# Layer 0's first stage: row normalisation with Newton's inverse root on VectorE instead of a square root on ScalarE

## The chip, the cores and the metric

One core of a Trainium2 chip runs the whole program. The metric is the device time of one launch in microseconds, the median of several runs.

## The reference, cut to what matters

Two layers, each a graph block and a block of eight experts with two chosen per token, over x of 128 x 64 x 128 (8192 tokens of 128 numbers). What the change touches is the end of layer 0's graph block, the normalisation behind it, and the routing:

```python
def _layernorm(x, axis=-1, eps=1e-05):
    m = jnp.mean(x, axis=axis, keepdims=True)
    v = jnp.var(x, axis=axis, keepdims=True)
    return (x - m) / jnp.sqrt(v + eps)

x = x + _L0_gnn_ref(_layernorm(x), adj, W1, b1, W2, b2)   # U (relu((U^T x) W1 + b1) W2 + b2), U: eigenvectors
x = x + _L0_ffn_ref(_layernorm(x), router_w, w1, w2, w3)
# _L0_ffn_ref: logits = flat @ router_w.T; softmax; top_k of 2; gates renormalised (+ 1e-9);
#              out = sum of the gates times w2 (silu(w1 x) * w3 x) of the two experts
x = x + _L1_gnn_ref(_layernorm(x), adj, ...)
x = x + _L1_ffn_ref(_layernorm(x), ...)
```

## The kernel before, in words

The eigenvectors of the graph's Laplacian are computed first (to about 291 us). Then comes the stage of the change, `gnn0_*`, which runs over 16 tiles (`TILES`) of 512 tokens, each tile four blocks (`PAIRS`) of 128 rows. It is a software pipeline of 21 steps (`A0_STEPS`). Each engine has its own list, written out by hand for every step `s`, and runs it strictly in order; semaphores tie the lists together.

- TensorE in step s: the multiplication with U^T (L1192) for tile s; the counting of a routing group (`count`, L948 and L949); w2 (L1201) for tile s-1; the transposes (L1209) of the normalised tile s-3, which wait for `a0_xh2`; w1 (L1215) for tile s; the output multiplication with U (L1220) for tile s-1; the logits (L861) of tile s-3.
- ScalarE in step s: first the square root (L1232) of the variance of tile s-2, then the copies out of PSUM: `ga` (L1237), `gm` (L1242), `xT` (L1247), then the Relu `gh` (L1252), and in every second step the Exp of the gates (L937, L939).
- VectorE in step s: the reciprocal of the root (L1321) and the scaling (L1270, four instructions) of tile s-2; the residual add (L1280, from PSUM) of tile s-1, its `bn_stats` (L1287) and `bn_aggr` (L1295), and the variance plus epsilon (L1301). With `T = s-2` and `T1 = s-1`, `old` and `new` say whether these tiles exist.
- GpSimd: the 16 additions of a bias row (L1367), then the sends: one indirect DMA (L1012) for each of the 64 blocks of rows, which scatters the normalised rows to their slots in memory. `scatter` waits for the slots and the gates of a group; up to group 4 `rest` also waits for `a0_xadd` and `a0_xT` of later steps. SP issues nothing in this stage; it waits for all 64 sends before it loads the first expert tile.

The routing works in eight groups of two tiles (`GROUPS`, `GT`). Steps 5, 7, ... 19 are *choosing* steps: `choose` is a chain of 13 links on small operands (128 x 64 or 128 x 128), each of which waits for the one before it on VectorE's own semaphore; the kernel hands it a function `beside(k)` that puts other instructions behind link k, ahead of the wait for it. At its end stands `picked` (L923), for which the count on TensorE waits. Steps 6, 8, ... 20 are *placing* steps: `place` takes the slots from the count, and `gates` the gates, again with `beside`. Steps 0 to 4 have no routing.

```python
def due(s, lag):
    g, rest = divmod(s - lag, GT)
    return [g] if rest == 0 and 0 <= g < GROUPS else []
```

After the stage come the 71 expert tiles of layer 0, then layer 1, whose routing uses the same `Router` and whose normalisation keeps its square root.

Of the kernel before, what the change touches and what calls it, by code (L numbers as in the profile page):

```python
# [6 lines left out]
I32 = mybir.dt.int32  # L7
# [828 lines left out]
class Router:  # L836
# [114 lines left out]
    def place(self, dve, own, g):  # L951
# [6 lines left out]
        n1 = own.inc(V.tensor_tensor(r["a"], self.rank[:, 0:one], r["o1"], ALU.mult))  # L958
        n2 = own.inc(V.tensor_tensor(r["b"], self.rank[:, (self.ways - 1) * one:self.ways * one], r["o2"], ALU.mult))
        dve.wait_ge(own.sem, n1)  # L960
        with self.nc.allow_low_precision(reason="whole numbers below 2**24"):
            V.tensor_reduce(self.t["slot"][:, 0, qs], group(r["a"]), AX.X, ALU.add).then_inc(s("slots"), 1)
            dve.wait_ge(own.sem, n2)
            V.tensor_reduce(second[:, qs], group(r["b"]), AX.X, ALU.add).then_inc(s("slots"), 1)

# [160 lines left out]

def first_norm_sum(nc, act, S, E, t, i):
# [129 lines left out]
def gnn0_dve(nc, dve, own, S, t, ps, route):  # L1257
# [4 lines left out]
    for s in range(A0_STEPS):  # L1262
# [4 lines left out]
        def scaled(q):  # L1267
            if not old:
                return
            ins = V.tensor_scalar(t["pay"][:, T * PAIRS + q, 0:P], X[:, T * PAIRS + q, :], t["mv"][:, q, 0:1],  # L1270
                                  t["sd"][:, 2, q:q + 1], ALU.subtract, ALU.mult)
            if q == PAIRS - 1:
                ins.then_inc(S("a0_xh2"), 1)

# [14 lines left out]
        def moments(q):  # L1289
            if not new:  # L1290
                return
            if q == 0 and old:
                dve.wait_ge(S("a0_xh2"), T + 1)
            dve.wait_ge(S("a0_stats"), T1 * PAIRS + q + 1)
            V.bn_aggr(t["mv"][:, q, :], t["bn"][:, q, :]).then_inc(S("a0_moments"), 1)  # L1295

        def variance():
# [15 lines left out]
        def by_gates(k):  # L1313
            if k == 0:
# [4 lines left out]
        if old:  # L1319
            dve.wait_ge(S("a0_root"), T + 1)  # L1320
            own.chain(V.reciprocal(t["sd"][:, 2, :], t["sd"][:, 1, :]))  # L1321
        if due(s, GT + 3):
            route.choose(dve, own, due(s, GT + 3)[0], by_choice)
            moments(3)
            variance()
        else:
            for q in range(PAIRS):
                scaled(q)
            if due(s, GT + 4):
                route.place(dve, own, due(s, GT + 4)[0])  # L1330
                route.gates(dve, own, due(s, GT + 4)[0], by_gates)
            else:
                added()
                for q in range(PAIRS - 1):
                    stats(q)
            stats(PAIRS - 1)
            for q in range(PAIRS):
                moments(q)
            variance()
# [644 lines left out]
def build(nc, d, out, scratch):  # L1984

    with ExitStack() as ctx:
# [45 lines left out]
        t["bn"], t["mv"], t["sd"] = sb("bn", [P, PAIRS, 6]), sb("mv", [P, PAIRS, 2]), sb("sd", [P, 3, PAIRS])  # L2032
        nm = sb("norm", [P, 2, 2, PAIRS])
# [191 lines left out]
```

## Time and profile before

| what | value |
|---|---|
| timed runs, us | 1470.77, 1477.38, 1479.84; median 1477.38 |
| span of the profiled execution, us | 1487.3 |
| instructions | 23954 |
| busy: TensorE, VectorE, ScalarE, GpSimd | 76%, 61%, 39%, 44% |
| mean granted clock of TensorE | 0.919 |

The profiled execution is one run of its own; its span goes from the first to the last instruction. The busy shares are means over the whole program; the stage in question is a small part of it, about 292 to 449 us.

### The profile page before, as it was taken

To read this page: it belongs to the slowest core of one execution; us is meant where nothing else is said; L and a number is where in the kernel's file an instruction comes from. 1 tells how busy PE (TensorE), PEld (TensorE's weight loads), DVE (VectorE), ACT (ScalarE), POOL (GpSimd) and SP (SyncE) were. 2 spreads that over 40 slices of the span, in tenths; PEclk is the share of its full clock that TensorE was granted. 3 is DMA by queue.
4 is the path that set the end of the run, shared out by engine and by line. 5 is a ranking of instruction groups with operands and counts; after the bars stand their busy time and mean duration, and the time that the engine had idled before them with its cause. 6 is when DMAs were issued, how large, how long until landed. Compare 5 with 4: busy or idle time off the path is not lost.

```text
span 1487.3 us, 23954 instructions
## 1 busy us (share of the span) xinstructions
PE 1130.7 (76%) x6500; PEld 939.8 (63%) x6500; DVE 904.2 (61%) x3700; ACT 574.8 (39%) x1601; POOL 655.7 (44%) x675
## 2 busy tenths in 40 slices
PE   4555685488716877889999587899878877799990
PEld 3555674366615766668888443677657666699990
DVE  5776788667753534446677687888434423355673
ACT  3556566045411211112222266577523322244440
POOL 3000000145565665655444770044456656556654
PEclk9999999989856988899999799899999979799995
DMA  9993000001112221222243330001112212122436
GB/s 228 428 427 132 1 1 1 0 1 33 37 43 62 68 65 56 62 59 63 64 117 108 117 127 15 1 31 34 33 49 68 67 55 64 61 70 69 131 106 226
DMA packets 59269, 125.57 MB, mean 84 GB/s; under 512 B 13132, under 2 KB 39637, under 8 KB 57600
## 3 DMA queue, kind: packets, MB, share of 16 engines
q0 software_dynamic: 20000, 73.21, 13.1%
q1 hardware_dynamic: 39136, 50.84, 12.6%
q8 instruction: 53, 0.87, 0.2%
q14 instruction: 80, 0.66, 0.1%
HBM read 50.83 MB, written 74.99 MB: 85 GB/s over the span
## 4 chain that ended last, share of the span: by engine, by line
PE 56%; issue 15%; DVE 14%; another core or an unknown queue 5%; ACT 5%; DMA 2%; POOL 1%; DVEq 0%; SPq 0%; ACTq 0%; POOLq 0%
PE bank L1583 15%; PE bank L1574 9%; PE bank L1572 6%; PE bank L1571 6%; PE bank L1796 3%; PE bank L195 3%; PE bank L1804 3%; PE bank L1751 2%; PE bank L1559 2%; DMA u<-planes 1%; DVE bnh L1648 1%; DVE u L180 1%; DVE u L171 1%; DVE bn L1119 1%
## 5 line engine op out<-in xcount | busy, mean ns | idle before, releaser
L1426 POOL DMA_INDIRECT planes<-work,goal x284 | 301.5, 1062 | 217.0 <-DVE work L1495 133.0
L1012 POOL DMA_INDIRECT rows<-pay,slot x256 | 259.5, 1014 | 259.9 <-issue 82.9
L1583 PE MATMUL bank<-pay 128*128 128x128 f32 (+1 forms) x1988 | 297.9, 290 | 61.2 <-issue 25.7
L1583 PEld LDWEIGHTS bank<-pay 128*128 128x128 f32 (+1 forms) x1988 | 273.0, 200 | 89.1 <-issue 36.1
L1543 ACT ACTIVATE pay<-bank,pay 128x256 f32<-128x256 f32 x284 | 126.6, 475 | 214.7 <-PE bank L1574 119.9
L1539 ACT ACTIVATE pay<-bank 128x256 f32<-128x256 f32 (+1 forms) x213 | 80.7, 383 | 311.2 <-PE bank L1572 216.5
L1574 PE MATMUL bank<-pay 128*128 128x256 f32 x568 | 145.3, 402 | 10.1 <-issue 8.8
L1571 PE MATMUL bank<-pay 128*128 128x256 f32 (+1 forms) x426 | 138.2, 408 | 12.9 <-issue 12.3
L1516 DVE TENSOR_TENSOR pay<-pay,bank 128x256 f32<-128x256 f32 (+1 forms) x213 | 88.2, 418 | 95.4 <-ACT pay L1539 58.3
L1572 PE MATMUL bank<-pay 128*128 128x256 f32 (+1 forms) x426 | 135.6, 402 | 0.0
L1574 PEld LDWEIGHTS bank<-pay 128*128 128x128 f32 x568 | 109.9, 204 | 25.2 <-issue 10.2
L195 PE MATMUL bank<-u 63*64 63x2 f32 (+61 forms) x496 | 73.6, 255 | 67.2 <-DVE u L180 66.2
L1468 DVE COPY pay<-wreg 128x1066 f32 (+1 forms) x142 | 103.3, 727 | 27.3 <-issue 26.7
L1478 DVE COPY pay<-bank 128x256 f32<-128x256 f32 x142 | 59.7, 421 | 83.7 <-remote 55.7
L195 PEld LDWEIGHTS bank<-u 63*64 63x64 f32 (+61 forms) x496 | 64.4, 217 | 72.7 <-DVE u L180 71.4
L1572 PEld LDWEIGHTS bank<-pay 128*128 128x128 f32 (+1 forms) x426 | 81.6, 192 | 19.4 <-issue 1.4
L1571 PEld LDWEIGHTS bank<-pay 128*128 128x128 f32 (+1 forms) x426 | 76.1, 193 | 27.0 <-issue 15.9
L1804 PE MATMUL bank<-wreg,work 128*128 128x128 f32 x512 | 69.6, 282 | 20.4 <-ACT work L1863 17.5
L1804 PEld LDWEIGHTS bank<-wreg,work 128*128 128x128 f32 x512 | 63.4, 194 | 31.6 <-ACT work L1863 22.3
L1490 DVE TENSOR_TENSOR pay<-bank,pay 128x256 f32<-128x256 f32 x71 | 30.1, 424 | 75.4 <-PE bank L1583 51.8
L714 POOL MEMSET work<- 128x868 f32 x1 | 0.8, 822 | 166.4 <-DVE u L350 166.4
L1796 PE MATMUL bank<-u,wreg 128*128 128x512 f32 x128 | 65.9, 618 | 0.0
(409 smaller groups left out, 2006.6 us busy)
## 6 DMA issues: line engine op xcount, KB each, us to landing
rows<-pay POOLq DMA_DIRECT2D x10, 3432.0 KB, 56.1
pay<-rows SPq DMA_DIRECT2D x142, 130.0 KB
u<-planes SPq DMA_DIRECT2D x64, 256.0 KB, 4.9
planes<-work,goal POOLq DMA_INDIRECT x284
wreg<-in_w SPq DMA_DIRECT2D x1, 4264.0 KB, 24.9
wreg<-in_w SPq DMA_DIRECT2D x1, 4112.0 KB, 13.2
X<-in_x SPq DMA_DIRECT2D x2, 2048.0 KB, 20.4
rows<-pay,slot POOLq DMA_INDIRECT x256
```

Source lines behind the costliest of these rows:

```text
L195: T.matmul(out, A[0:rows, col:col + 1].to_broadcast([rows, N]), rhs, start=True, stop=True).then_inc(hp, 1)
L1012: return self.nc.gpsimd.indirect_dma_start(out=xs, out_offset=bass.IndirectOffsetOnAxis(ap=self.t["slot"][:, k, q:q + 1], axis=0), in_=sel ...
L1426: nc.gpsimd.indirect_dma_start(out=planes, out_offset=bass.IndirectOffsetOnAxis(ap=t["goal"][:, j * 2 + h:j * 2 + h + 1], axis=0), in_=t[" ...
L1468: V.tensor_copy(t["wst"][j % 2][:, 0:WB[layer]], W[:, bass.ds(expert * WB[layer], WB[layer])]).then_inc(s("w"), 1)
L1516: V.tensor_tensor(t["hh"][c][0:w, :], t["hs"][c][0:w, :], ps[c][0:w, TS:2 * TS], ALU.mult).then_inc(s("hh"), 1)
L1543: A.activation(t["hh"][c], ps[c][:, 0:TS], ACT.Gelu, bias=t["wst"][j % 2][:, 2 * CH1 * P + c:2 * CH1 * P + c + 1]).then_inc(s("hh"), 1)
L1571: T.matmul(ps[c][0:n, 0:TS], w[:, a:a + n], x, start=True, stop=True)
L1572: T.matmul(ps[c][0:n, TS:2 * TS], w[:, HID0 + a:HID0 + a + n], x, start=True, stop=True).then_inc(s("up"), 1)
L1574: T.matmul(ps[c][:, 0:TS], w[:, c * P:(c + 1) * P], x, start=True, stop=True).then_inc(s("up"), 1)
L1583: ins = T.matmul(ps[4 + j % 2][:, h * P:(h + 1) * P], t["hh"][c][0:n, h * P:(h + 1) * P], t["wst"][j % 2][0:n, at + c * P:at + (c + 1) * P ...
L1796: T.matmul(ps[2 + c % 2][:, :], t["WS"][:, c * P:(c + 1) * P], t["x1"][i], start=True, stop=True).then_inc(S("a1_up"), 1)
L1804: ins = T.matmul(ps[4 + 2 * (i % 2)][:, q * P:(q + 1) * P], t["sh"][c][:, q * P:(q + 1) * P], t["WS"][:, (CH1 + c) * P:(CH1 + c + 1) * P], ...
```

## The change

In layer 0's first stage the square root on ScalarE and the reciprocal on VectorE are replaced by a bit-pattern start value and three Newton steps, 11 small operations (128 x 4) on VectorE per tile: operation 0 takes the place of the variance plus epsilon at the end of the step, operations 1 to 10 stand in the next step. In a choosing step they go behind links 0 to 9, in a placing step behind the operations of `place` and `gates`, in steps without routing one behind the other ahead of the add. The four scalings move to behind links 10 to 12, or to the end of the step; the four `bn_aggr` move to the very end and write into two buffers in turn.

```diff
+ROOT_OPS = 11
+SEED = 0x5f3759df - (1 << 22) - (1 << 31)
+
+def inverse_root(V, dve, t, sem, n, k, mv=None):
+    mv = t["mv"] if mv is None else mv
+    half, y, q = (t["sd"][:, i, :] for i in range(3))
+    if k:
+        dve.wait_ge(sem, n * ROOT_OPS + k)
+    if k == 0:
+        ins = V.tensor_scalar(half, mv[:, :, 1], EPS, 0.5, ALU.add, ALU.mult)
+    elif k == 1:
+        ins = V.tensor_scalar(t["sdi"][:, 1, :], t["sdi"][:, 0, :], -0.5, float(SEED), ALU.mult, ALU.add)
+    elif k % 3 == 2:
+        ins = V.tensor_tensor(q, y, y, ALU.mult)
+    elif k % 3 == 0:
+        ins = V.tensor_tensor(q, q, half, ALU.mult)
+    else:
+        ins = V.scalar_tensor_tensor(out=y, in0=q, scalar=-1.5, in1=y, op0=ALU.add, op1=ALU.mult)
+    ins.then_inc(sem, 1)
...
 def gnn0_act(nc, act, S, t, ps, route):
...
-        if 2 <= s < TILES + 2:
-            act.wait_ge(S("a0_var"), s - 1)
-            A.activation(t["sd"][:, 1, :], t["sd"][:, 0, :], ACT.Sqrt).then_inc(S("a0_root"), 1)
...
         def scaled(q):
...
+            if q == 0:
+                dve.wait_ge(S("a0_inv"), (T + 1) * ROOT_OPS)
+            ins = V.tensor_scalar(t["pay"][:, T * PAIRS + q, 0:P], X[:, T * PAIRS + q, :], t["mvs"][T % 2][:, q, 0:1],
+                                  t["sd"][:, 1, q:q + 1], ALU.subtract, ALU.mult)
...
+        def root(k):
+            if old and 1 <= k < ROOT_OPS:
+                inverse_root(V, dve, t, S("a0_inv"), T, k)
...
         def variance():
...
             dve.wait_ge(S("a0_moments"), (T1 + 1) * PAIRS)
-            V.tensor_scalar(t["sd"][:, 0, :], t["mv"][:, :, 1], EPS, None, ALU.add).then_inc(S("a0_var"), 1)
+            if old:
+                dve.wait_ge(S("a0_xh2"), T + 1)
+            inverse_root(V, dve, t, S("a0_inv"), T1, 0, t["mvs"][T1 % 2])
 
         def by_choice(k):
-            if k <= 3:
-                scaled(k)
-            elif k == 5:
+            root(k + 1)
+            if k == 5:
                 added()
             elif 6 <= k <= 9:
                 stats(k - 6)
-            elif k >= 10:
-                moments(k - 10)
+            elif k == 10:
+                scaled(0)
+                scaled(1)
+            elif k >= 11:
+                scaled(k - 9)
+
+        def by_place(k):
+            root(k + 2)
 
         def by_gates(k):
+            root(k + 6)
             if k == 0:
                 added()
             else:
                 stats(k - 1)
 
-        if old:
-            dve.wait_ge(S("a0_root"), T + 1)
-            own.chain(V.reciprocal(t["sd"][:, 2, :], t["sd"][:, 1, :]))
         if due(s, GT + 3):
             route.choose(dve, own, due(s, GT + 3)[0], by_choice)
-            moments(3)
-            variance()
-        else:
+        elif due(s, GT + 4):
+            root(1)
+            route.place(dve, own, due(s, GT + 4)[0], by_place)
+            route.gates(dve, own, due(s, GT + 4)[0], by_gates)
+            root(10)
+            stats(PAIRS - 1)
             for q in range(PAIRS):
                 scaled(q)
...
+        else:
+            for k in range(1, ROOT_OPS):
+                root(k)
+            added()
             for q in range(PAIRS):
-                moments(q)
-            variance()
+                stats(q)
+            for q in range(PAIRS):
+                scaled(q)
+        for q in range(PAIRS):
+            moments(q)
+        variance()
```

`place` gets the same argument `beside` as `gates` has, and calls it behind each of its four operations.

## Rows read from the trace of the kernel before

**Rows 1.** GpSimd's sends, the view of line L1012 and GpSimd's order of time.

```profile
L1012 POOL DMA_INDIRECT rows<-pay,slot x64: 969/974/1592, 339.0 to 446.9; - x64
...
410.28 0.97 POOL L1012 DMA_INDIRECT rows<-pay,slot  x1 [0.30 <-issue]
...
437.35 1.59 POOL L1012 DMA_INDIRECT rows<-pay,slot  x1 [6.88 <-issue]
```

**Rows 2.** VectorE in order of time, at its longest wait.

```profile
428.45 0.22 DVE L873 COPY rt<-bank 128x64 f32<-128x64 f32 x1 [9.41 <-remote]
```

**Rows 3.** All engines in order of time, step 7's add to step 8's.

```profile
341.83 0.68 DVE L1280 TENSOR_TENSOR X<-X,bank 128x512 f32<-128x512 f32 x1
...
345.09 0.26 DVE L923 TENSOR_TENSOR rt<-rt,carry 128x128 f32<-128x128 f32 x1
...
345.41 0.49 PE L948 MATMUL bank<-rt,kroute 128*128 128x128 f32 x2 [1.97 <-DVE rt L923]
...
345.79 0.57 ACT L1237 COPY u<-bank 128x512 f32<-128x512 f32 x1
...
347.29 1.02 PE L1215 MATMUL bank<-u,small 128*128 128x512 f32 x2
...
348.14 1.02 PE L1220 MATMUL bank<-u,UTB 128*128 128x512 f32 x2
...
349.20 0.69 DVE L1280 TENSOR_TENSOR X<-X,bank 128x512 f32<-128x512 f32 x1 [1.17 <-PE bank L1220]
```

**Rows 4.** VectorE in order of time, from step 6's add to step 7.

```profile
336.30 0.69 DVE L1280 TENSOR_TENSOR X<-X,bank 128x512 f32<-128x512 f32 x1 [2.56 <-PE bank L1220]
...
338.73 0.17 DVE L1301 TENSOR_SCALAR sd<-mv 128x4 f32<-128x4 f32 x1
339.17 0.18 DVE L1321 RECIPROCAL sd<-sd 128x4 f32<-128x4 f32 x1 [0.27 <-ACT sd L1232]
339.39 0.22 DVE L873 COPY rt<-bank 128x64 f32<-128x64 f32 x1
```

**Rows 5.** Waits from 290 to 450 us: total, times, longest.

```profile
PE bank L1215 <- ACT u L1237: 5.9, 6, 2.4
```

**Rows 6.** Busy time of each engine in one stretch, granted clock.

```profile
core 0: us, PE busy (x) PEld busy (x) DVE busy (x) ACT busy (x) POOL busy (x), PEclk, DMA share, GB/s
...
329.00:410.30 81.30, 63.72 (x364) 49.38 (x362) 61.51 (x330) 41.65 (x75) 39.97 (x41) 0.92 0.10 33
```

**Rows 7.** VectorE in order of time, the links of step 7.

```profile
341.38 0.27 DVE L889 TENSOR_TENSOR rt<-rt,rc 128x64 f32<-128x64 f32 x1
341.69 0.22 DVE L892 SCALAR_TENSOR_TENSOR rt<-rt 128x64 f32<-128x64 f32 x1
...
342.80 0.15 DVE L898 TENSOR_TENSOR rc<-rc 128x8 f32<-128x8 f32 x1
342.87 0.27 DVE L899 TENSOR_TENSOR rt<-rt,rc 128x64 f32<-128x64 f32 x1
...
343.94 0.26 DVE L908 TENSOR_TENSOR rt<-rt,rc 128x64 f32<-128x64 f32 x1
...
344.24 0.42 DVE L915 TENSOR_TENSOR_SCAN rt<-kroute,rt 128x128 f32<-128x128 f32 x1
...
344.69 0.29 DVE L918 TENSOR_TENSOR rt<-rt 128x128 f32<-128x128 f32 x1
...
346.13 1.12 DVE L1270 TENSOR_SCALAR pay<-X,mv,sd 128x128 f32<-128x128 f32 x4
347.17 0.22 DVE L958 TENSOR_TENSOR rt<-bank,rt 128x64 f32<-128x64 f32 x1
```

**Rows 8.** VectorE in order of time, steps 2 and 5.

```profile
304.75 4.47 DVE L1270 TENSOR_SCALAR pay<-X,mv,sd 128x128 f32<-128x128 f32 x4
...
327.53 0.68 DVE L1280 TENSOR_TENSOR X<-X,bank 128x512 f32<-128x512 f32 x1
```

**Rows 9.** ScalarE in order of time, a table load and the next root.

```profile
386.99 1.28 ACT L1232 ACT_TABLE_LOAD   x1
388.28 0.20 ACT L1232 ACTIVATE sd<-sd 128x4 f32<-128x4 f32 x1
```

More of the change, by code:

```diff
@@ L949, in count, with place @@
         T.matmul(self.rank, ones, r["e"][:, 0:self.ways * E8 * GQ], start=False, stop=True).then_inc(self.s("rank"), 1)
-    def place(self, dve, own, g):
+    def place(self, dve, own, g, beside=lambda k: None):
         V, r, s, c = self.nc.vector, self.t["rt"], self.s, self.t["rc"]
@@ L958, in place @@
         n1 = own.inc(V.tensor_tensor(r["a"], self.rank[:, 0:one], r["o1"], ALU.mult))
+        beside(0)
         n2 = own.inc(V.tensor_tensor(r["b"], self.rank[:, (self.ways - 1) * one:self.ways * one], r["o2"], ALU.mult))
+        beside(1)
         dve.wait_ge(own.sem, n1)
@@ L962, in place @@
             V.tensor_reduce(self.t["slot"][:, 0, qs], group(r["a"]), AX.X, ALU.add).then_inc(s("slots"), 1)
+            beside(2)
             dve.wait_ge(own.sem, n2)
             V.tensor_reduce(second[:, qs], group(r["b"]), AX.X, ALU.add).then_inc(s("slots"), 1)
+            beside(3)
     def gates(self, dve, own, g, beside=lambda k: None):
@@ L1269, in scaled @@
                 return
-            ins = V.tensor_scalar(t["pay"][:, T * PAIRS + q, 0:P], X[:, T * PAIRS + q, :], t["mv"][:, q, 0:1],
-                                  t["sd"][:, 2, q:q + 1], ALU.subtract, ALU.mult)
+            if q == 0:
+                dve.wait_ge(S("a0_inv"), (T + 1) * ROOT_OPS)
+            ins = V.tensor_scalar(t["pay"][:, T * PAIRS + q, 0:P], X[:, T * PAIRS + q, :], t["mvs"][T % 2][:, q, 0:1],
+                                  t["sd"][:, 1, q:q + 1], ALU.subtract, ALU.mult)
             if q == PAIRS - 1:
                 ins.then_inc(S("a0_xh2"), 1)
+        def root(k):
+            if old and 1 <= k < ROOT_OPS:
+                inverse_root(V, dve, t, S("a0_inv"), T, k)
         def added():
@@ L1291, in moments @@
                 return
-            if q == 0 and old:
-                dve.wait_ge(S("a0_xh2"), T + 1)
+            if q == 0 and T1 >= 2:
+                dve.wait_ge(S("a0_xh2"), T1 - 1)
             dve.wait_ge(S("a0_stats"), T1 * PAIRS + q + 1)
-            V.bn_aggr(t["mv"][:, q, :], t["bn"][:, q, :]).then_inc(S("a0_moments"), 1)
+            V.bn_aggr(t["mvs"][T1 % 2][:, q, :], t["bn"][:, q, :]).then_inc(S("a0_moments"), 1)
         def variance():
@@ L1317, in by_gates @@
                 stats(k - 1)
-        if old:
-            dve.wait_ge(S("a0_root"), T + 1)
-            own.chain(V.reciprocal(t["sd"][:, 2, :], t["sd"][:, 1, :]))
         if due(s, GT + 3):
             route.choose(dve, own, due(s, GT + 3)[0], by_choice)
-            moments(3)
-            variance()
-        else:
+        elif due(s, GT + 4):
[4 more added lines that the diff above has]
+            stats(PAIRS - 1)
             for q in range(PAIRS):
                 scaled(q)
[L1329 to L1336, printed above, removed]
-            for q in range(PAIRS):
-                moments(q)
-            variance()
+        else:
+            for k in range(1, ROOT_OPS):
+                root(k)
+            added()
+            for q in range(PAIRS):
+                stats(q)
[4 more added lines that the diff above has]
+        variance()
 def clear_rows(nc, pool, S, zeros, xs):
@@ L2032, in build @@
         t["bn"], t["mv"], t["sd"] = sb("bn", [P, PAIRS, 6]), sb("mv", [P, PAIRS, 2]), sb("sd", [P, 3, PAIRS])
+        t["sdi"] = t["sd"][:, :, :].bitcast(I32)
+        t["mvs"] = [t["mv"], sb("mv_odd", [P, PAIRS, 2])]
         nm = sb("norm", [P, 2, 2, PAIRS])
```

## The prediction

> **What bounds the kernel now.** I read four views in turn: the sends of GpSimd, the order of time of all engines over two steps, the order of time of VectorE alone, and the table of waits.
>
> The stage hands over to the experts when the last of the 64 first sends has landed. The sends run from 339.0 to 446.9 us, the 41st (group 5) at 410.28 [rows 1]. Up to group 4 GpSimd is held at the pace of the pipeline by its waits on `a0_xadd` and `a0_xT`; from group 5 on it has no such waits, and a send costs 0.97 us plus 0.30 idle, 1.28 us. 24 sends need 30.7 us. So the end of the stage is the moment at which group 5 may start, plus 30.7, plus one gap of 6.88 us before group 7 [rows 1]. That gap comes from one wait of VectorE for the last logits, 9.41 us with a releaser that the profile doesn't know [rows 2]. Everything then turns on the pace of the steps. I measure it from one add of L1280 to the next; both paths below pass through it.
>
> *From the add of a choosing step to the next one* (341.83 to 349.20, 7.37 us) [rows 3]: add, links 6 to 12 of the routing, `picked` at the end of L923 (345.35); TensorE's count starts at 345.41, then w2, transposes, w1 (347.29) and the output matmul (starts 348.14, ends 349.16); VectorE adds at 349.20. ScalarE's copy `ga`, the one that stands behind the square root, ends at 346.36, 0.93 us before the w1 matmul of 347.29 that reads it. The square root isn't on this path.
>
> *From the add of a placing step to the next* (336.30 to 341.83, 5.53 us) [rows 3, 4]: VectorE alone, no wait on TensorE at its end: variance at 338.73, ScalarE's root, reciprocal at 339.17, the choice from 339.39, its link 5 at 341.83. In two of the pairs this path took 1.5 us more with late signals from TensorE; I leave it out on both sides.
>
> ScalarE holds TensorE up elsewhere: w1 waited for `ga` 5.9 us in six times [rows 5]. In the stretch 329 to 410.3 us VectorE was busy 61.51 of 81.30 us, ScalarE 41.65, GpSimd 39.97 [rows 6]. VectorE is the fullest engine beside TensorE, and it lies on both paths.
>
> **The change, part by part.** Removed: per tile one root on ScalarE, one reciprocal and one wait of VectorE, and the switches between the tables of Sqrt and Exp. Added: 11 operations of 128x4 per tile in place of two, 9 x 16 = 144 more on VectorE. Moved: the four scalings from links 0 to 3 (or the head of a step) to links 10 to 12 (or the end). SP issues nothing here and GpSimd's list is unchanged, waits included. The trace has no operation of the Newton steps; the nearest rows are small ones: L898 (128x8) took 0.15 us and put the next instruction off by 0.07 [rows 7]; with a second input scalar I take 0.12. A small operation that waits for the one before costs 0.22 (339.17 to 339.39) [rows 4]. Where a link is alone, its successor waits 0.31 (L889 to L892) for an occupancy of 0.18 [rows 7], so a root operation there is free. Bounds of one are thus 0 and 0.22 us.
>
> *Choosing step, add to add.* Links 6 to 9 already have a `bn_stats` beside them and leave no gap: root operations 7 to 10 add 0.12 + 0.07 + 0.07 + 0.12 = 0.38. One scaling occupies 0.26 (four of them put L958 off by 1.04, 346.13 to 347.17) [rows 7]. Link 10: L908 to L915 is 0.30; with two scalings 0.17 + 0.52 = 0.69, so +0.39. Link 11: L915 to L918 is 0.45; with one scaling 0.34 + 0.26 = 0.60, +0.15. Link 12: L918 to L923 is 0.40 with a `bn_aggr` of 0.09 in it; 0.31 + 0.26 = 0.57, +0.17 [rows 3, 7]. The `bn_aggr` leave these links, which is counted in the differences. Sum: 1.09 us later `picked`, and count, w2, transposes, w1 and output follow one to one: 7.37 becomes 8.46. Behind `picked` nothing waits for the later `a0_xh2`: TensorE's transposes stand behind the count.
>
> *Placing step, add to add.* The wait for the root and the reciprocal go: 338.73 to 339.39 is 0.66, of which 0.10 stays for root operation 0: -0.56 [rows 4]. Four scalings leave links 0 to 3, which then run at their own latency: -0.53 (each falls from about 0.41 to 0.28). They come back at the end of the placing step, which VectorE must finish before the next choice: +1.04. Root operations 7 to 10 stand between the gates' links beside `bn_stats`: +0.38; operation 6 of the next tile ahead of the add: +0.07. Operations 1 to 6 and the slots lie in time in which VectorE waited for the output matmul (1.17 us at 349.20) [rows 3], so nothing; without that cover 0.5 us. Sum +0.40: 5.53 becomes 5.93. TensorE is next in line at the same time: it now waits for `a0_xh2` at about 3.5 us behind the add, then transposes 0.44, w1 0.86, output 1.04, 5.9.
>
> So a pair of steps grows by 1.49 us. From the add of step 6 to that of step 16, whose gates open group 5, lie five pairs: +7.4 us.
>
> *Front, steps 2 to 4.* Ten root operations run one after the other ahead of the add: 2.2 us. In step 2 the output matmul is waited for anyway, and the slow scalings against GpSimd's additions (4.47 us for four) [rows 8] move behind the add; step 3's scalings fall behind the end of GpSimd's additions and cost 1.04 in place of 2.5. Summing VectorE's steps so gives the add of step 5 between 325.2 and 329.0 in place of 327.53 [rows 8]; -2.3 to +1.5. I take -1.0, nearer to the low end, since only two of the root operations have a form that GpSimd held up. *Behind step 16* nothing: GpSimd's 24 sends cover the last three groups, as long as group 7 is ready in time; its late signal [rows 2] I leave as it is. *Links to the gates of group 5*: roots 7 to 10 in step 16, +0.3 before the gates.
>
> Sum: +7.4 - 1.0 + 0.3 = +6.7 us, and the experts and all that follows shift by the same. Against the profiled execution's own 1487.3 us that is 1494.0. That execution lies 9.9 us above the median of the three timed runs, 1477.38; the shift belongs to both: 1484.1.
>
> *A rule of the skill.* VectorE's small operations cost next to nothing in data and 0.07 us in the row [rows 7]. The Trainium skill, VectorE: DVE Perf Modes, section on the TRN2 errata, says that an SBUF operand costs a fixed number of cycles per instruction (58 + elements at 0.96 GHz, by estimate 65 ns here); this speaks against the change, and 144 of them are 9.3 us if nothing hides them. The trace agrees in size; 6 of the 11 places hide it.
>
> **The rivals.** (a) *ScalarE in front of TensorE was the brake.* For it: VectorE sets ScalarE free only at the end of a step, and w1 waited 5.9 us for `ga` [rows 5]. If those go whole, and the late signal with its gap of 6.88 us doesn't come again [rows 1], the time falls by 12.8: 1464.6. Against it: both paths above pass ScalarE by. (b) *The table switches.* Loads take 1.28 us; at 386.99 one ended at 388.27 and the root started at 388.28 [rows 9]. Six switches to the root's table and six back vanish; were each on the path, 12 x 1.28 = 15.4 us: 1462.0. Against: the five others ended 0.9 us or more before the variance came. The skill's ScalarE: Activation LUTs, section What ACT_TABLE_LOAD costs, adds a drain of 1380 ns to each switch, by estimate 16.6 us more; the row at 388.28 shows none. (c) *Slower by over 1%: root operations exposed.* Each waits for the one before on the same semaphore engine, and the links behind it in VectorE's queue wait too. If none hides, (11 x 0.22 - 0.66) x 16 = 28 us; half of that, 14, with 1.2 us a pair for the moved scalings, 6: 1497. It decides if a link with its root takes over 0.45 us. (d) *Nothing moves:* GpSimd's pacing swallows it. Against it stands that its idle time is the pipeline's. 1477.
>
> **How the numbers follow.** Forecast (slower by 3 to 12 us) 0.60; (a) 0.13; (b) 0.04; (c) 0.11; (d) 0.12. The likeliest gives 1484. The range reaches down into (a), to 1469, and up to 1493: front at its worse end (+2.5), and TensorE's clock at half for longer, since it idles longer before each count. The stretch of [rows 6] was granted 0.92; by estimate a window at half clock adds up to 1.9 us to a choosing step, since count, w2 and transposes take 1.88 us (345.41 to 347.29) [rows 3]. Beyond 1% (14.8 us), about what a measurement of this kernel can tell from no change, lie (b), a little of (a), and (c): faster 0.06, same 0.82, slower 0.12.
>
> **What would show it.** L923 to the add before it 4.3 us in place of 3.3 in choosing steps; adds in pairs of about 8.5 and 5.9 us; no table load of L1232's kind; ScalarE idle before its copies for TensorE, no longer for VectorE; GpSimd's group 5 near 417. Wrong would make it: root operations that take the links' latency without adding any; scalings that pass faster at links 10 to 12; a choice whose `picked` isn't what TensorE waits for; or the gap before group 7 gone, which alone gives 6.9 us back.

## The result, and the profile after

| | before | after |
|---|---|---|
| device time, median (lowest to highest) | 1474.86 us (1470.77 to 1479.84), 4 runs | 1495.57 us (1487.0 to 1500.6), 4 runs |
| span of the profiled execution | 1487.3 us | 1485.2 us (its own time 1487.0) |
| same kernels on another chip | 1476.51 us, 25 runs | 1497.32 us, 4 runs |

The changed kernel is slower, by a ratio of 1.012 with a 95% interval of 1.008 to 1.016 (17.7 us; the two medians differ by 20.7); on another chip the ratio was 1.014 (1.009 to 1.020). The prediction said 1484 and a range up to 1493, and the measured median lies 2.6 us above that range.

The two profiled executions of the first comparison point the other way (1487.3 before, 1485.2 after), and that is the first thing to learn from them. The span of before lies 12 us over its kernel's median, and a kernel's own time is 1.8 us more than its span, so 14 us in all; the one of after is the fastest of its four. A span is not the measurement. Each kernel was therefore profiled once more, on one chip: spans of 1471.9 and 1497.4 us. The excess of the first lies behind this stage: from the last send to the end it took 1040.4 us, against 1027.5 in the second profile of the same kernel and 1028.2 and 1034.2 in the two of the changed one.

First the page of the changed kernel: span, busy time by engine, and the granted TensorE clock in tenths in 40 slices (one is 37 us; the stage lies in slices 9 to 12).

```profile
span 1485.2 us, 24077 instructions
...
PE 1135.9 (76%) x6500; PEld 941.5 (63%) x6500; DVE 918.9 (62%) x3844; ACT 559.5 (38%) x1573; POOL 655.1 (44%) x675
...
PEclk9999999988866998999999799799999978899995
```

The slices 9 to 11, at 8 tenths, are the steps of the pipeline. The same in stretches, cut where the granted clock changes (us of each engine, then the clock):

```profile
core 0: us, PE busy (x) PEld busy (x) DVE busy (x) ACT busy (x) POOL busy (x), PEclk, DMA share, GB/s
...
382.00:389.00 7.00, 6.20 (x20) 4.78 (x21) 2.76 (x21) 1.84 (x3) 3.23 (x4) 0.53 0.09 29
389.00:399.00 10.00, 7.22 (x49) 5.67 (x47) 9.23 (x56) 3.40 (x8) 4.73 (x5) 0.99 0.11 36
399.00:406.00 7.00, 6.05 (x20) 4.69 (x21) 2.91 (x21) 1.69 (x3) 3.25 (x4) 0.52 0.09 29
```

7 us at half (1.2 GHz), 10 at full (2.4 GHz), 7 at half: one period is one pair of steps, 17.0 us, and it repeats from 364.7 to 422.8. Over the stage up to group 5 (329.00 to 425.40) the grant was 0.84, against 0.92 in [rows 6] and 0.88 in the second profile of before (329.00 to 412.86). What stands in a half-clock stretch is seen in all engines' order of time, from one add of L1310 (L1280 before) to the next; it answers to [rows 3]:

```profile
378.25 0.69 DVE L1310 TENSOR_TENSOR X<-X,bank 128x512 f32<-128x512 f32 x1
...
378.86 1.14 PE L1219 MATMUL bank<-UB,pay 128*128 128x128 f32 x8
...
382.46 0.28 DVE L923 TENSOR_TENSOR rt<-rt,carry 128x128 f32<-128x128 f32 x1
...
382.80 0.80 PE L948 MATMUL bank<-rt,kroute 128*128 128x128 f32 x2 [2.80 <-DVE rt L923]
...
383.82 1.92 PE L1228 MATMUL bank<-small,u 128*128 128x128 f32 x8
...
385.52 1.06 PE L1236 MATMUL bank<-consts,pay 128*128 128x128 f32 x4
...
386.38 1.92 PE L1242 MATMUL bank<-u,small 128*128 128x512 f32 x2
...
388.08 1.30 PE L1247 MATMUL bank<-u,UTB 128*128 128x512 f32 x2
...
389.42 0.69 DVE L1310 TENSOR_TENSOR X<-X,bank 128x512 f32<-128x512 f32 x1 [4.12 <-PE bank L1247]
```

`picked` comes 4.21 us behind the add, nearly as predicted (4.3). But TensorE waited 2.80 us for it where it had waited 1.97 in [rows 3], and then the matmuls ran at half the clock: count to add is 6.62 us instead of 3.79. The step takes 11.17 us where 8.46 was predicted.

The same trace has a choosing step at full clock, the first one:

```profile
335.74 0.49 PE L948 MATMUL bank<-rt,kroute 128*128 128x128 f32 x2 [2.81 <-DVE rt L923]
...
339.54 0.69 DVE L1310 TENSOR_TENSOR X<-X,bank 128x512 f32<-128x512 f32 x1 [1.80 <-PE bank L1247]
```

Here TensorE had waited 2.81 us too, the grant was 1.00 from 329 to 345 us, and from add 5 (331.19) to add 6 it took 8.35 us, the predicted length. The wait of 2.8 us did not bring the half clock every time; where the half clock came, the step took up to 2.8 us more.

The second place is the front. VectorE in order of time, from the first tile's variance to step 2's add, and GpSimd in the same stretch:

```profile
303.90 1.34 DVE L1142 TENSOR_SCALAR sd<-mv 128x4 f32<-128x4 f32 x1
305.27 1.19 DVE L1144 TENSOR_SCALAR sd<-sd 128x4 int32<-128x4 int32 x1
306.50 1.19 DVE L1146 TENSOR_TENSOR sd<-sd 128x4 f32<-128x4 f32 x1
...
308.94 1.18 DVE L1150 SCALAR_TENSOR_TENSOR sd<-sd 128x4 f32<-128x4 f32 x1
...
312.59 1.18 DVE L1150 SCALAR_TENSOR_TENSOR sd<-sd 128x4 f32<-128x4 f32 x1
313.81 0.16 DVE L1146 TENSOR_TENSOR sd<-sd 128x4 f32<-128x4 f32 x1
...
314.28 0.69 DVE L1310 TENSOR_TENSOR X<-X,bank 128x512 f32<-128x512 f32 x1
```

```profile
295.36 18.39 POOL L1405 TENSOR_TENSOR X<-X,work 128x512 f32<-128x512 f32 x15
```

While GpSimd adds the bias (until 313.75), eight root operations of 128x4 in a row take 1.18 to 1.34 us each, every form of them; the ninth takes 0.16. The add of step 2 comes at 314.28, and that of step 5 at 331.19 against 327.53 in [rows 8].

At the end of the stage, GpSimd's sends: the 64 in one line, then group 5's first and group 7's first, which answer to [rows 1].

```profile
L1016 POOL DMA_INDIRECT rows<-pay,slot x64: 964/972/1554, 342.4 to 457.0; - x64
...
425.40 0.97 POOL L1016 DMA_INDIRECT rows<-pay,slot  x1 [1.02 <-issue]
...
447.51 0.97 POOL L1016 DMA_INDIRECT rows<-pay,slot  x1 [1.71 <-issue]
```

Group 5 starts at 425.40 instead of 410.28, 15.1 us later where 6.7 had been predicted. The last send comes only 10.1 us later, because the gap before group 7 is 1.71 instead of 6.88 us. The second pair of profiles shows how the gap varies between executions:

| | add 5 | add 6 | add 16 | group 5 | gap before group 7 | last send |
|---|---|---|---|---|---|---|
| before, first profile | 327.53 | 336.30 | 407.53 | 410.28 | 6.88 | 446.92 |
| before, second | 328.70 | 337.55 | 410.20 | 412.86 | 1.65 | 444.44 |
| after, first | 331.19 | 339.54 | 422.64 | 425.40 | 1.71 | 457.02 |
| after, second | 331.69 | 342.65 | 426.85 | 429.61 | 3.62 | 463.20 |

In the second pair the last send is 18.8 us later, and the medians on that chip differ by 20.8, so nearly all of the loss is made in this stage.

### The profile page after: what moved, and what is told of

Its sections match the earlier page's. It is cut to its first block, busy times and chain, and to the rows that moved or that the text cites. A ratio compares the mean times of both kernels' runs of the same rounds, so it can differ in the third digit from the quotient of the medians.

```text
span 1485.2 us, 24077 instructions
## 1 busy us (share of the span) xinstructions
PE 1135.9 (76%) x6500; PEld 941.5 (63%) x6500; DVE 918.9 (62%) x3844; ACT 559.5 (38%) x1573; POOL 655.1 (44%) x675
## 4 chain that ended last, share of the span: by engine, by line
PE 60%; DVE 20%; issue 8%; ACT 4%; another core or an unknown queue 3%; DMA 2%; POOL 1%; DVEq 0%; SPq 0%; POOLq 0%; ACTq 0%
PE bank L1621 15%; PE bank L1612 9%; PE bank L1609 6%; PE bank L1610 6%; PE bank L195 3%; PE bank L1834 3%; PE bank L1842 3%; PE bank L389 3%; PE bank L1789 2%; PE bank L1597 2%; DMA u<-planes 1%; DVE bnh L1686 1%; DVE u L180 1%; DVE u L171 1%
## 5 line engine op out<-in xcount | busy, mean ns | idle before, releaser
L1621 PE MATMUL bank<-pay 128*128 128x128 f32 (+1 forms) x1988 | 293.5, 287 | 51.9 <-issue 34.3
L1621 PEld LDWEIGHTS bank<-pay 128*128 128x128 f32 (+1 forms) x1988 | 268.5, 197 | 79.7 <-issue 44.2
L1610 PEld LDWEIGHTS bank<-pay 128*128 128x128 f32 (+1 forms) x426 | 81.2, 191 | 19.0 <-issue 0.8
L1609 PEld LDWEIGHTS bank<-pay 128*128 128x128 f32 (+1 forms) x426 | 75.7, 192 | 26.1 <-issue 15.0
## 6 DMA issues: line engine op xcount, KB each, us to landing
wreg<-in_w SPq DMA_DIRECT2D x1, 4112.0 KB, 13.2
```

The costliest lines, as they stand in the source:

```text
L1609: T.matmul(ps[c][0:n, 0:TS], w[:, a:a + n], x, start=True, stop=True)
L1610: T.matmul(ps[c][0:n, TS:2 * TS], w[:, HID0 + a:HID0 + a + n], x, start=True, stop=True).then_inc(s("up"), 1)
L1621: ins = T.matmul(ps[4 + j % 2][:, h * P:(h + 1) * P], t["hh"][c][0:n, h * P:(h + 1) * P], t["wst"][j % 2][0:n, at + c * P:at + (c + 1) * P ...
```

## The experiments

The kernels ran in three groups, each on one chip with runs of the kernel before (medians 1474.9, 1335.8 and 1476.5 us). The kernel before took 10% less time on the second chip. In the profiles taken there the last send comes as early or late as on the other chips and the time behind it is shorter (894 to 898 us against 1026 to 1040); so ratios go by the kernel before on the same chip, and between chips only times within this stage are compared. The kernel before was not profiled on the second chip. "Choosing" and "placing" are the distances from the add of a choosing or placing step to the next add, from add 6 to add 15; "add 6 to 16" are the five pairs. The step from add 15 to add 16 is left out of the third column: it ran at half clock in most profiles (8.34 us in before, 10.26 in after), and the fill kernels have no filler there.

| kernel | ratio to before (95%) | choosing, us | placing, us | add 6 to 16 | last send |
|---|---|---|---|---|---|
| *chip 1* | | | | | |
| before | | 7.37 to 9.44 | 5.53 to 7.08 | 71.2 | 446.9 |
| after | 1.012 (1.008 to 1.016) | 10.03 to 11.17 | 5.85 | 83.1 | 457.0 |
| front_old | 1.011 (1.006 to 1.015) | 11.08 to 11.19 | 5.86 | 84.2 | 457.0 |
| after_fill | 1.006 (1.003 to 1.010) | 9.03 to 9.09 | 5.87 | 76.0 | 451.6 |
| added_alone | 1.006 (1.003 to 1.009) | 9.06 to 10.66 | 6.1 to 6.2 | 78.2 | 459.1 |
| moved_alone | 1.008 (1.004 to 1.012) | 8.06 and 9.72 | 6.4 to 6.6 | 77.9 | 453.4 |
| *chip 2* | | | | | |
| before_fill | 0.995 (0.993 to 0.998) | 7.38 | 5.54 | 65.5 | 433.4 |
| before_count_late | 0.990 (0.985 to 0.995) | 6.61 | 5.53 | 60.2 | 427.3 |
| after_count_late | 0.999 (0.997 to 1.000) | 7.22 | 5.9 to 6.1 | 66.4 | 439.9 |
| after_small_bias | 1.008 (1.005 to 1.011) | 11.15 to 11.30 | 5.9 | 84.6 | 448.7 |
| *chip 3* | | | | | |
| before_again | 0.999 (0.996 to 1.003) | 7.37 to 9.88 | 5.5 to 6.9 | 72.7 | 444.4 |
| after_again | 1.014 (1.009 to 1.020) | 11.08 to 11.18 | 5.85 | 84.2 | 463.2 |
| after_front_old_count_late | 1.003 (1.000 to 1.006) | 7.21 | 5.9, 7.8 to 10.0 | 79.3 | 448.2 |
| moved_count_late | 1.004 (1.000 to 1.007) | 7.49 | 6.6, 7.4 | 72.9 | 448.8 |

**front_old.** The changed kernel, with the first three tiles' roots as before (BY_ROOT = 3; the first hunk stands in `gnn0_act`, the second in `variance`):

```
+        if 2 <= s < BY_ROOT + 2:
+            act.wait_ge(S("a0_var"), s - 1)
+            A.activation(t["sd"][:, 1, :], t["sd"][:, 0, :], ACT.Sqrt).then_inc(S("a0_root"), 1)
...
+            if T1 < BY_ROOT:
+                V.tensor_scalar(t["sd"][:, 0, :], t["mvs"][T1 % 2][:, :, 1], EPS, None, ALU.add).then_inc(S("a0_var"), 1)
```

> The changed kernel, but tiles 0 to 2 (steps 2 to 4, ahead of the routing) go by the root on ScalarE and the reciprocal, with the scalings at the head of the step, as before. Theory A (in the front the small operations wait one by one for GpSimd's additions, 1.19 us each instead of 0.16): the add of step 2 comes at about 309 us instead of 314.3, that of step 5 at about 327.5 instead of 331.2; the stage and the whole program end 3 to 5 us earlier than the changed kernel's. Rival (the front catches up, since the pipeline behind it is bound by the choosing steps): the add of step 5 moves, the whole by less than 1 us. The pairs of steps behind the front stay at 5.9 and 11.1 us by both.

The add of step 5 came at 328.50, 2.7 us earlier; but from there to add 6 it took 10.96 us instead of 8.35, so add 6 stood at 339.46 (339.54 in the changed kernel) and the last send where it had been. So far the rival was right. (The median of front_old, 1486.9 us, lies 8.7 us below the changed kernel's, but the intervals of the two ratios overlap.) One row of stretches shows where the gain went:

```profile
331.60:338.40 6.80, 5.35 (x19) 4.32 (x20) 3.28 (x23) 1.17 (x2) 0.00 (x0) 0.50 0.02 4
```

What the front gave back, a half-clock stretch between add 5 and add 6 took. The changed kernel itself has that stretch in its second profile (10.96 us) and not in its first. The front's loss is real but is not simply added to that of the pairs.

**after_fill.** The changed kernel; TensorE multiplies into an unused bank while it would wait for the choosing, ahead of five of the counts (steps 6, 8, ... 14):

```
+            if s < TILES:
+                for _ in range(10):
+                    T.matmul(ps[6][:, P:2 * P], t["w2g0"], t["w2g0"], start=True, stop=True)
             route.count(pe, g)
```

> The changed kernel with ten 128x128 multiplications on TensorE ahead of each count (7 times), whose result nobody reads; they fill the 2.8 us in which TensorE waits for the choice. Theory B (TensorE's clock falls to half behind the long wait, and count, w2, transposes, w1 and output then take 6.6 instead of 3.8 us): the granted clock between 340 and 425 us stays near 1, the path from the add of a choosing step to the next falls from 11.1 to about 8.4 us, the whole program gets 10 to 14 us shorter than the changed kernel. Rival (VectorE's longer list binds and the clock is a bystander): the clock rises, the path stays at 10 to 11 us, the whole stays within 2 us of the changed kernel or gets longer by the filler.

```profile
379.49 0.49 PE L948 MATMUL bank<-rt,kroute 128*128 128x128 f32 x2 [0.45 <-DVE rt L923]
...
380.04 1.06 PE L1231 MATMUL bank<-small,u 128*128 128x128 f32 x8
...
382.20 0.59 ACT L1269 COPY u<-bank 128x512 f32<-128x512 f32 x1 [4.77 <-PE bank L1231]
```

```profile
329.00:408.50 79.50, 68.25 (x453) 53.55 (x451) 66.27 (x412) 28.24 (x56) 36.35 (x36) 1.00 0.10 31
```

Nothing on VectorE was changed, and every half-clock stretch up to 408.5 is gone. w2's four matmuls take 1.06 us instead of 1.92, and add 6 to add 16 takes 76.0 us instead of 83.1. The filler doesn't delay the count: TensorE still waits 0.45 to 0.60 us for `picked`. From add 5 to add 6 it took 8.36 us, as expected (8.4); the later filled steps took 9.03 to 9.09, because ScalarE's copy of w2's result started 1.1 us after w2's modelled end there, a late signal (above: w2 ends at 381.10, the copy starts at 382.20). So the clock gave back 7.1 us, and 2.8 more would be gained without the late signals. The whole is 10.5 us shorter by the medians, 8 by the ratios; 10 to 14 had been expected.

**added_alone** and **moved_alone.** The kernel before with one half of the change each. The first keeps ScalarE's root and the scalings where they were, and computes the eleven Newton operations beside them into a tile that nobody reads (`root(k + 1)` in `by_choice`, and the changed kernel's calls in `by_place`, `by_gates` and ahead of the add):

```
+        t["nd"] = sb("nd", [P, 3, PAIRS])
...
+            root(k + 1)
```

> The kernel before, with the eleven small operations added in the same places as in the change, on a tile of their own that nobody reads; root, reciprocal and scalings as before. Theory (ports in the front, 0.38 us in the links): the add of step 2 moves back by 5 us or more, the choosing step's add to picked grows from 3.5 to 3.9 us, the placing step's path by 0.4 to 0.5 us; with the clock falling in some of the pairs the whole gets 8 to 16 us longer than before. Rival (the moved scalings are what costs): under 3 us longer.

The second keeps Sqrt and reciprocal, and moves scalings and moments to the places of the changed kernel:

```
-            if k <= 3:
-                scaled(k)
+            if k == 10:
+                scaled(0)
+                scaled(1)
+            elif k >= 11:
+                scaled(k - 9)
```

> The kernel before, with root and reciprocal as before, but the four scalings behind links 10 to 12 or at the end of the step, and the moments behind them in two buffers, as in the change. Theory (scalings lengthen links 10 to 12 by 0.7 us, TensorE waits 2.6 us for the count and its clock falls): add to picked 4.2 us, the path from a choosing step's add to the next 8.1 us at full clock and 10 to 11 us at half, the whole 6 to 12 us longer than before; the front like before. Rival (only the added operations cost): within 3 us of before.

Of the 11.9 us that the whole change cost over five pairs, the first half alone costs 7.0 and the second 6.6 (the two don't add up to the whole), and both show a half clock in choosing steps (six stretches of 3.4 to 6.8 us between 337 and 423 us in the first, four between 336 and 418 in the second). With the scalings at the step's end and the root still on ScalarE, VectorE's list stands idle for the root at the head of each step, as before, and has the scalings behind it; placing steps take 6.4 to 6.6 us.

Both halves also lose in the front. Add 5 comes at 334.64 in added_alone and at 331.16 in moved_alone, against 327.53 in before. For moved_alone "the front like before" was expected, and that missed: add 3 came at 319.32 instead of 315.06. Ahead of it four scalings took 3.97 us beside GpSimd's additions, and VectorE then waited 4.02 us for TensorE; how the two hang together was not followed up:

```profile
310.38 3.97 DVE L1270 TENSOR_SCALAR pay<-X,mv,sd 128x128 f32<-128x128 f32 x4
...
319.32 0.69 DVE L1280 TENSOR_TENSOR X<-X,bank 128x512 f32<-128x512 f32 x1 [4.02 <-PE bank L1220]
```

Both are slower by what had been expected (by the ratios 9 and 12 us), and the rivals, under 3 us, are out. At the links, a `picked` that came 0.3 us later (3.55 behind the add, added_alone) or 0.7 us later (3.92, moved_alone) cost 1.3 to 1.4 us a pair in all. Part of that is VectorE's own work in placing steps (6.1 to 6.6 us instead of 5.5); with the half-clock stretches it points at TensorE's wait, and not at the root operations as such.

**after_count_late** and **before_count_late.** In `gnn0_pe` the count moves from its place ahead of w2 to behind the transposes:

```
-        for g in due(s, GT + 4):
-            route.count(pe, g)
         if 1 <= s <= TILES:
             pe.wait_ge(S("a0_gh"), s)
...
             ins.then_inc(S("a0_t"), 1)
+        for g in due(s, GT + 4):
+            route.count(pe, g)
```

> The changed kernel with TensorE's two matmuls of the count put behind the transposes of their step instead of ahead of the second layer's matmuls. The choosing of a group then no longer holds up the matmuls between two additions. Theory (a wait for the choosing, lengthened by root operations at its links, keeps TensorE idle for 2.8 us and its clock falls to half for the matmuls behind it): the distance from a choosing step's addition to the placing step's falls from 11.1 us to 6.5 to 7.5, no half-clock window between 320 and 400, add 16 near 403 to 408 instead of 422.6, the sends' end 10 to 14 us earlier than 457.0, the whole 1475 to 1480 us. Rival (VectorE's longer chain alone is what costs, wherever TensorE stands): the distance stays over 10 us and the whole over 1485.

> The same move of the count in the kernel before. Theory: there too the count's wait lies on the way from a choosing step's addition to the next; 7.37 to 8.34 us become about 6.1, five pairs give 5 to 7 us, the whole about 1469. Rival: the step is bound by VectorE's own work (6 us busy of each), and the time stays within 0.3% of the kernel before.

The changed kernel, TensorE and VectorE in order of time, and its stretch:

```profile
377.19 0.66 PE L1234 MATMUL bank<-consts,pay 128*128 128x128 f32 x4 [1.72 <-DVE pay L1296]
377.68 0.39 PE L948 MATMUL bank<-rt,kroute 128*128 128x128 f32 x2
...
380.05 0.69 DVE L1310 TENSOR_TENSOR X<-X,bank 128x512 f32<-128x512 f32 x1 [0.43 <-PE bank L1247]
```

```profile
325.60:404.00 78.40, 62.62 (x403) 48.87 (x403) 71.61 (x440) 32.67 (x61) 36.90 (x37) 1.00 0.10 32
```

The wait before the count is gone. TensorE now waits 1.72 us for the scalings, with w2 done meanwhile; the clock is whole; the add waits 0.43 us instead of 4.12. The choosing step took 7.22 us and add 16 came at 406.93, both as expected; the last send came 17.1 us earlier than in the changed kernel, more than the 10 to 14 expected. This edit does two things at once: it restores the clock, and it takes the wait for `picked` off the way to the add, so its gain (83.1 to 66.4 us) is more than the clock's. The changed kernel is level with the kernel before. And the kernel before gains by the same edit:

```profile
370.37 0.69 DVE L1280 TENSOR_TENSOR X<-X,bank 128x512 f32<-128x512 f32 x1 [0.39 <-PE bank L1220]
```

```profile
320.00:398.30 78.30, 67.57 (x425) 51.67 (x423) 68.46 (x364) 47.62 (x88) 40.69 (x41) 1.00 0.11 35
```

Expected was a gain of 5 to 7 us; it is 12 us, 1.0% (0.5 to 1.5). By its ratio this is the fastest version of all. What the change costs in this order of the code is read between these two, with the clock whole in both up to the last step: five pairs 66.4 against 60.2 us, 1.22 us a pair, and 6.6 us at add 6 (340.57 against 333.93), nearly all of it from the front (add 5 at 333.35 against 327.32; on this chip the changed kernel's front ran at half clock from 308 to 325, longer than the 310 to 320 of its first profile).

**before_fill.** Six matmuls of that kind in the kernel before.

> The kernel before with six idle 128x128 matmuls ahead of the count's wait, so that TensorE has work in the wait. In the kernel before the clock was at half for three windows between 313 and 406 us. Theory: with the clock at full, additions 3 to 14 come 1 to 4 us earlier in all, the whole 0 to 3 us less. Rival: the six matmuls (about 0.35 us at full clock) are late themselves and cost what the clock gives: within 1 us of no change.

Full clock from 320.4 to 395.5; five pairs 65.5 us instead of 71.2 and 72.7, ratio 0.995. So the kernel before, too, was losing to this wait. Not all of the 5.7 us between the two profiles is the clock, though: two placing steps of 7.1 us and a choosing step of 7.97 in before, 3.6 us over their usual length in all, ran at full clock with late signals of TensorE, which no step of before_fill shows; one choosing step at half clock (9.44 us) makes up the other 2.1. The filler here took about 1.4 us and not 0.35, and still ended before `picked` came. The half-clock stretches of the kernel before were in its trace ahead of the prediction.

**after_small_bias.** GpSimd adds one column of 128 of the bias for all tiles but the first; the rest of the bias is left out.

```
+            nc.gpsimd.tensor_tensor(xt[:, :, 0:1], xt[:, :, 0:1], pairs(t["b2mixed"])[:, :, 0:1], ALU.add).then_inc(S("a0_pre"), 1)
```

> The changed kernel with GpSimd's additions of the output bias cut to one column of 128 for all tiles but the first (the bias is left out of the other columns; the other work is the same). Theory (GpSimd's additions hold up VectorE's small operations one by one, 1.18 to 1.34 us each): the root operations of steps 1 and 2 take 0.2 us each as in later steps, so that addition 2 comes near 304 to 306 instead of 314.3, addition 5 near 322 to 325 instead of 331.2, and the later pairs stay at 17.0 us. Rival (the slow operations of the front wait for their own inputs or for a cold start of VectorE's chain): they stay at 1.2 us, addition 2 at 312 or later.

```profile
304.61 0.16 DVE L1146 TENSOR_TENSOR sd<-sd 128x4 f32<-128x4 f32 x1
...
306.26 0.69 DVE L1310 TENSOR_TENSOR X<-X,bank 128x512 f32<-128x512 f32 x1
```

```profile
295.92 2.04 POOL L1408 TENSOR_TENSOR X<-X,work 128x4 f32<-128x4 f32 x13
```

GpSimd is done at 298.0 and the root operations take 0.16 us, 0.20 apart. Add 2 comes at 306.26 instead of 314.28, add 5 at 321.5 instead of 331.19. From add 5 to add 6 it took 10.04 us, with a half-clock stretch, instead of 8.35, so 8.0 of the 9.7 us are left at add 6. The pairs behind keep their length and their half clock, as expected: the two losses are separate causes. Without the additions the kernel before might gain in its front as well (its four scalings of step 2 took 4.47 us beside them [rows 8]); that was not run, so 9.7 us is not the price of the root operations.

**before_again** and **after_again**, both kernels profiled once more:

> The kernel before, unchanged, profiled a second time. Theory (the stall of 6.88 us ahead of group 7's sends and the late ends of TensorE's work in the profiled execution of before were of that execution alone, whose own time was 12 to 14 us over the median): the last send ends at 437 to 441 us instead of 446.9, and the choosing-to-placing distances are 7.4 and 8.3 without the 8 to 9.4 of steps 8 to 13. Rival (the stall belongs to the kernel): the last send near 447 again, with the gap ahead of group 7.

> The changed kernel, unchanged, profiled a second time. Theory: the same additions as in its first profile within 1 us (its half-clock windows came in every pair and hang on its own waits), last send at 455 to 459 us; its time is 16 to 20 us over the kernel before on the same chip, which is the difference of the last sends once the kernel before is without its stall. Rival (the times of the first comparison were of its runs): ratio to the kernel before below 1.008.

The gap before group 7 of the kernel before is 1.65 us this time, so that part of the theory holds (the changed kernel has gaps of 1.71 and 3.62); the rest doesn't. Late choosing steps of 9.0 and 9.9 us are there again, in other pairs, and the last send is at 444.4, not 437 to 441. Add 16 is even 2.7 us later than in the first profile. The changed kernel's last send came at 463.2, above the band, with half clock already between add 5 and add 6 (10.96 us); its time is 20.8 us over the kernel before, at the upper end of the 16 to 20 expected.

**after_front_old_count_late** and **moved_count_late**:

> The changed kernel with the first three tiles' roots by ScalarE's Sqrt and a reciprocal, and with the count behind the transposes. Theory (front and count's wait are the two large costs; what is left of the change is the links' own price, 1.0 to 1.2 us a pair): addition 5 at 326 to 329, pairs of 13.1 to 13.3 us, addition 16 at 401 to 404, last send 3 to 4 us ahead of the run that moves the count alone (439.9), the ratio to the kernel before 0.993 to 0.998. Rival: the front's gain is lost at step 6 as in the run that restored the front alone (ratio as that of the count alone, 0.9985).

> The kernel before with the scalings and moments moved to the step's end as in the change, ScalarE's Sqrt kept, and the count behind the transposes. Theory (with the clock at full the move costs what stands at the links): no half-clock window from 320 to 398, pairs of 12.5 to 13.5 us against 12.14 with the count late in the kernel before and 13.2 in the changed one, last send 430 to 437, ratio 0.992 to 0.998. Rival (scalings at the end hold up the transposes and these the count, now behind them): pairs over 14 us, ratio over 1.

Both missed. With the scalings moved and the root still on ScalarE, the late count leaves pairs of 14.1 to 14.9 us at whole clock, as the rival had it. With old front and late count the choosing steps are 7.21 us as hoped, but the placing steps take 7.8 to 10.0 instead of 5.9. TensorE and VectorE there:

```profile
383.95 0.66 PE L1234 MATMUL bank<-consts,pay 128*128 128x128 f32 x4 [0.94 <-issue]
386.88 2.08 PE L1242 MATMUL bank<-u,small 128*128 128x512 f32 x2 [2.27 <-ACT u L1267]
```

```profile
390.42 0.69 DVE L1317 TENSOR_TENSOR X<-X,bank 128x512 f32<-128x512 f32 x1 [4.02 <-PE bank L1247]
```

ScalarE's copy (L1267) started at 386.25, although the matmuls that it reads end at 382.1 by their rows: their signal came at 386.22, and the signals of three groups of matmuls within 0.2 us. The matmuls behind such a wait then run at half clock (L1242 takes 2.08 us instead of 1.02): the grant is at half around 369 to 373, 386 to 390 and 403 to 407 us, although the count stands late. after_count_late, on chip 2, has no such late signal in any pair. Whether this belongs to the chip or to the order of the code was not told apart, since the two kernels didn't run on one chip. So the level result of after_count_late, and the 1.0% of before_count_late, stand for chip 2 alone.

## Why the prediction missed

The direction was right and the size was off: +6.7 us predicted at the start of group 5, 15.1 and 16.8 measured; +6.7 in the whole, 17.7 by the ratio. The step that failed is the one behind `picked` in a choosing step, which was put at TensorE's full clock; a term of the front had the wrong sign besides. Point by point:

- *The paths.* Right. The choosing step runs through `picked`, count and TensorE (the add waits 4.12 us for L1247), the placing step through VectorE alone, with no wait at its add. ScalarE's root was on neither: with it gone, nothing got faster. Rivals (a) and (b) are out. At the routing's links the root operations stayed hidden as far as predicted (add to `picked` 4.21 against 4.3), so (c) is out there, though its time, 1497, was near the outcome by luck; only in the front did they lie open.
- *Placing step.* 5.93 predicted, 5.85 measured in both profiles. The prediction left the late signals of two placing steps "out on both sides"; the changed kernel doesn't have them, so 3.1 us stood on one side alone. Over the five pairs the placing steps got 1.4 us shorter (+2.0 predicted) and the choosing steps 13.2 us longer (+5.5 predicted).
- *Choosing step, the links.* +1.09 predicted. `picked` came 0.95 us later, and the one choosing step at full clock took 8.35 us (8.36 in after_fill) where 8.46 had been predicted. Of the two kernels with the late count the whole pair differs by 1.22 us, where 1.49 had been predicted for the count in its old place. The working was sound, "the trace agrees in size" apart: 0.07 us is what a small operation puts the next one off by where that doesn't wait for it; a root operation that waited for the one before came 0.20 us behind it.
- *Choosing step, "count, w2, transposes, w1 and output follow one to one".* This step failed. They follow, but at half clock: count to add 6.62 us instead of 3.79. The prediction had the cost in its range ("up to 1.9 us to a choosing step") from w2's and the transposes' rows only, and left it out of the sum. It is 2.83 us, because w1 and the output matmul slow down as well, and choosing steps of 11.1 us and more came three times in the first profile's five pairs, four times in the second's. A later `picked` thus costs its 0.95 us and, where the clock falls about the wait that it lengthens from 1.97 to 2.80 us, up to another 2.8. after_fill shows it: whole clock with VectorE untouched, 7.1 us less over five pairs. The trace of before had such a step as well (9.44 us, half clock from 385 to 392), so the price could have been read ahead.
- *The front.* -1.0 predicted within -2.3 to +1.5, measured +3.7 and +3.0 at add 5. In step 2 "the output matmul is waited for anyway" was wrong: add 2 of the kernel before stands right behind its scalings with no wait for TensorE, so what is put ahead of it shows in full as soon as it is longer than they were. And "only two of the root operations have a form that GpSimd held up" was wrong: eight in a row were held up, 1.18 to 1.34 us each, of all forms. I had the price of one (a scaling of 4.47 / 4) and judged by the form instead of the neighbour. The Trainium skill, SBUF — State Buffer, section "SBUF: two separate sides", says that VectorE and GpSimd share a port pair under an exclusive lock, which the one that starts first gets for its whole instruction; of VectorE's operations it names those in a two-port performance mode, and those with two SBUF inputs if GpSimd reads SBUF. The trace agrees for the operations with two inputs, 1.18 us for 128x4 beside additions of about 1.2 us each; those with one (`tensor_scalar`, 1.34 and 1.19 us) were held up too, and in which mode they ran no run here shows. after_small_bias shows GpSimd's additions to be the cause. The prediction read it as a price of large operations; here each small operation took about the time of one addition of GpSimd, so in proportion the smallest suffered most.
- *The late signal and its gap.* "I leave as it is": the gap of 6.88 us was 1.65 in the second profile. It stood in the base of a sum made against a profile that lies 14 us above its median, of which about 13 us lie behind the stage. This did not change the forecast's difference, but the two together hid the loss in the first comparison of spans.
- *The chances.* Slower by over 1% had 0.12, by way of (c), exposed root operations. The outcome came by another mechanism, which the text names and prices only as an edge of the range.

How it adds up to add 16, first profiles (second in brackets): up to add 6 +3.2 (+5.1), five pairs +11.9 (+11.6), in all +15.1 (+16.7). The pairs' 11.9 us split so: the four choosing steps of the changed kernel from add 7 to add 14 lie 10.0 us above the 8.36 us that such a step takes at full clock; the kernel before lost 2.1 us to its one step at half clock in that stretch and 3.6 us to late signals. What is left, 7.6 us, is VectorE's longer work, for which 7.4 had been predicted. With the count late on the second chip the same work costs 6.1 us (1.22 a pair).

## What to carry to other kernels

Before lengthening a chain that another engine waits for, read what that engine's clock does at the wait: with `picked` 0.95 us later the choosing steps got 2.6 us longer in the mean. An in-order queue should not hold its longest wait ahead of work that doesn't need it; moving two matmuls behind eight others gave 1.0% on its own, on one chip. Small operations weren't cheap beside GpSimd's large ones; and a sum should be made against a second profile if the first lies a per cent above the median.

## What was not expected of the hardware

- Dependent operations of 128x4 on VectorE came 0.20 us apart when nothing disturbed them and 1.22 when GpSimd added 128x512 tiles beside them. `bn_stats` and `bn_aggr` in the same stretch ran at 0.2 and 0.1 us each.
- Idle matmuls paid: ten in each of the filled choosing steps gave 7.1 us over the five pairs in the changed kernel (ratio 1.006 instead of 1.012); six gave a ratio of 0.995 in the kernel before.
- One chip ran the kernel before 10% faster than two others (1335.8 us against 1474.9 and 1476.5). From 466 to 830 us the DMA engines moved 93 GB/s there (after_count_late), against 70 and 77 in the kernel before on the other two. In before_fill, before_count_late and after_count_late, all on that chip, no step between add 6 and add 15 was longer than its like by more than 0.3 us. The cause of late signals (1.1 to 4 us, several within 0.2 us) stays open.
